# Score tiles by image in two attention stages, and dense matmuls ahead of every third group's scores

## What is computed

```python
# second attention (causal)
scores = jnp.einsum('bhqd,bhkd->bhqk', q, k) * (1.0 / math.sqrt(D))
scores = jnp.where(causal, scores, -jnp.inf)
att = jax.nn.softmax(scores, axis=-1)
y = jnp.einsum('bhqk,bhkd->bhqd', att, v)
# third attention (a scale for each head; a token doesn't look at itself)
attn = jnp.einsum('bhid,bhjd->bhij', q, k) * scale[None, :, None, None]
attn = jnp.where(diag[None, None, :, :], -jnp.inf, attn)
attn = jax.nn.softmax(attn, axis=-1)
out = jnp.einsum('bhij,bhjd->bhid', attn, v)
```

## Time and profile before

| | |
|---|---|
| median of 3 runs | 2166.01 us (2151.96 to 2166.42) |
| profiled execution | 2172.53 us |
| its span, first to last instruction | 2170.6 us |
| TensorE matmuls busy | 1868.5 us (86%), 12440 instructions |
| TensorE weight loads busy | 1723.5 us (79%) |
| VectorE busy | 1134.4 us (52%) |
| ScalarE busy | 799.2 us (37%) |
| GpSimd busy | 588.7 us (27%) |
| mean granted TensorE clock | 0.817 |
| DMA | 151.00 MB, mean 70 GB/s |

### The profile page before, as it was taken

One profiled execution on the slowest core, in us unless ns is written; L12 is line 12 of the kernel. 1 busy time (PEld: TensorE's weight loads), 2 busy tenths in 40 slices (PEclk: granted clock), 3 DMA queues, 4 the chain that ended last, 5 costly groups with the idle time before them and its releaser, 6 DMA issues.

```text
span 2170.6 us, 35211 instructions
## 1 busy us (share of the span) xinstructions
PE 1868.5 (86%) x12440; PEld 1723.5 (79%) x12440; DVE 1134.4 (52%) x3189; ACT 799.2 (37%) x1907; POOL 588.7 (27%) x1369
## 2 busy tenths in 40 slices
PE   7999999996938997998999888977998999889980
PEld 7999888876937777988898778876888898788870
DVE  2423245554327554675577643345775577643436
ACT  1211124323414333553454334434454454334420
POOL 3333241231046433123422310025313412310021
PEclk8855557657966656998998899998999999799995
DMA  4039400003420000001000046651001000046630
GB/s 117 18 107 286 138 1 15 14 24 91 163 78 23 1 15 27 1 1 56 15 2 14 27 139 199 210 170 33 4 1 55 16 1 14 13 150 203 203 107 28
DMA packets 77409, 151.00 MB, mean 70 GB/s; under 512 B 6344, under 2 KB 56626, under 8 KB 77141
## 3 DMA queue, kind: packets, MB, share of 16 engines
q1 hardware_dynamic: 70902, 136.49, 19.7%
q0 software_dynamic: 6336, 12.26, 2.0%
HBM read 108.67 MB, written 41.05 MB: 69 GB/s over the span
## 4 chain that ended last, share of the span: by engine, by line
PE 52%; issue 16%; DVE 14%; DMA 6%; POOL 4%; SPq 3%; ACT 3%; another core or an unknown queue 0%; DVEq 0%; POOLq 0%; ACTq 0%
PE ps_proj L1020 9%; PE ps_o L1075 7%; PE ps_pt L994 6%; DMA w_in<-w_all_dram 5%; PE ps_proj L1095 5%; PE ps_score L1053 4%; PE ps_proj L1033 4%; PE ps_score L1166 4%; PE ps_proj L1149 3%; PE ps_proj L947 2%; SPq L823 2%; ACT w_hi L1281 1%; PE ps_score L968 1%; DVE prob L1439 1%; DVE negmax L1438 1%
## 5 line engine op out<-in xcount | busy, mean ns | idle before, releaser
L1166 PE MATMUL ps_score<-w,hid 128*112 128x192 f32 (+2 forms) x1680 | 306.3, 335 | 14.1 <-DVE x L1717 6.2
L1166 PEld LDWEIGHTS ps_score<-w,hid 128*112 128x112 f32 (+2 forms) x1680 | 278.0, 180 | 16.8 <-issue 8.5
L1330 POOL TENSOR_SCALAR tmp<-rs,var 111x1 f32<-111x1 f32 x154 | 55.4, 360 | 855.9 <-DVE rs L1410 855.4
L1260 ACT ACTIVATE probt<-ps_pt 111x333 f32<-111x333 f32 x308 | 137.8, 447 | 338.7 <-PE ps_pt L994 336.6
L994 PE MATMUL ps_pt<-const,prob 111*111 111x111 f32 x924 | 198.8, 335 | 52.6 <-ACT probt L1260 40.6
L1271 ACT ACTIVATE hid<-ps_proj 128x224 f32<-128x224 f32 (+2 forms) x360 | 133.6, 382 | 265.9 <-PE ps_proj L1149 252.4
L994 PEld LDWEIGHTS ps_pt<-const,prob 111*111 111x111 f32 x924 | 150.0, 223 | 89.7 <-issue 54.5
L1075 PEld LDWEIGHTS ps_o<-v,probt 111*111 111x111 f32 x1584 | 213.5, 215 | 1.1 <-issue 0.5
L1075 PE MATMUL ps_o<-v,probt 111*111 111x65 f32 (+1 forms) x1584 | 208.1, 282 | 0.0
L1318 POOL DMA_INDIRECT tin<-rows_out,idx x66 | 68.0, 1030 | 499.8 <-issue 384.0
L1255 ACT ACTIVATE prob<-prob 111x333 f32<-111x333 f32 x308 | 145.8, 477 | 62.9 <-DVE prob L1439 57.6
(11 more groups left out here) (239 smaller groups left out, 4381.0 us busy)
## 6 DMA issues: line engine op xcount, KB each, us to landing
w_in<-w_all_dram SPq DMA_DIRECT2D x66, 768.0 KB, 4.4
w<-w_all_dram SPq DMA_DIRECT2D x50, 576.0 KB, 5.2
rows_in<-w_lo SPq DMA_DIRECT2D x1, 12320.0 KB, 64.5
rows_out<-w_lo SPq DMA_DIRECT2D x1, 9240.0 KB, 90.1
tin<-rows_in SPq DMA_DIRECT2D x36, 224.0 KB
rows_out<-tout SPq DMA_DIRECT2D x36, 168.0 KB
patch<-patches_dram SPq DMA_DIRECT2D x11, 333.0 KB, 3.2
wo<-wo_all_dram SPq DMA_DIRECT2D x6, 576.0 KB, 3.8
```

The lines of the kernel that those rows point to most:

```text
L1166: last = pe.matmul(bank[0:n, 0:C], hid[:, i % 2, m, at:at + n], w2[:, slot, m, :], start=(m == 0), stop=(m == FC - 1))
L1260: act.activation(probt[:, n % 4, :, :], ps_pt[0:TG, 0:3 * TG].rearrange("p (c n) -> p c n", c=3), ACT.Copy).then_inc(pt_taken, 1)
```

## The change

Both stages (`self.short`) get one score tile a group. The queries of a head are written three times as wide: for each group, image and half chunk, a block of 64 rows by 111 columns, in which columns h x 37 to (h + 1) x 37 hold the rows of head h and zeros elsewhere (a ScalarE copy with a scale that is zero on the other heads' rows). One product with the 37 keys of that image gives three heads' scores for it. So the tile is 111 rows (three heads of 37 queries) by 2 banks x 222 columns (half, image, key); nothing pairs tokens of different images. The probabilities need four transposes, the value products have 37 stationary columns and 51 moving ones (17 for each image, zero outside the token's own image), the outputs stand on 37 rows, and OT takes six transposes. Ahead of the scores of groups 1, 4, 7 and 10 TensorE does twelve products of 128 x 512 with whatever the weight buffer holds, into the bank that the mask then overwrites.

```diff
+        self.short = a in (CAUSAL, DIAG)
-        self.chunks = H // self.per_chunk
+        self.chunks = 2 if self.short else H // self.per_chunk
...
-        _n = 3 if ATTS[_st[1]].t5 else 2
+        _n = 3 if ATTS[_st[1]].t5 else 1
...
+def short_order(a, last_stage, follower):
+
+    out = first_block(a) if last_stage[0] == "ffn" else []
+    for n in range(G + 1):
+        slots = short_fill(a, n, last_stage, follower)
+        if n < G:
+            out.append(("S", n, 0))
+        out += slots[0]
+        if n:
+            out.append(("PV", n - 1, 1))
+        if n < G:
+            out.append(("E", n, 0))
+        out += slots[1]
+        if n < G:
+            out.append(("PT", n, 0))
+        if n:
+            out.append(("OT", n - 1, 0))
+        out += slots[2]
+        if n:
+            out.append(("Y", n - 1))
+        out += slots[3]
...
+                        if g % 3 == 1:
+
+                            full = w1_hi[:, LOAD0[st] % W_RING, :, :].rearrange("p c n -> p (c n)")
+                            for _ in range(12):
+                                pe.matmul(banks[0], full[:, 0:128], full[:, 0:512], start=True, stop=True,
+                                          skip_group_check=True)
                         for bank in banks:
-                            pe.matmul(bank[0:TG, 0:3 * TG], identb[:], maskb[:, a, :, :].rearrange("p h k -> p (h k)"),
+                            pe.matmul(bank[0:TG, 0:2 * TG], identb[:],
+                                      maskb[:, a, 0:2, :].rearrange("p h k -> p (h k)"),
                                       start=True, stop=False, skip_group_check=True)
+                        for j in range(2):
+                            for i in range(IPG):
+                                for e, bank in enumerate(banks):
+                                    at, col = 64 * e, (j * IPG + i) * NTOK
+                                    ins = pe.matmul(bank[0:TG, col:col + NTOK],
+                                                    short_q(b % 2)[at:at + 64, j, g - BLOCKS[b][0], i, :],
+                                                    short_k(b % 2)[at:at + 64, j, t0 + i * NTOK:t0 + (i + 1) * NTOK],
+                                                    start=False, stop=True, skip_group_check=True)
...
+                        for h in range(H):
+
+                            at = (h // 3 % 2 * 2 + h // 6) * TG + h % 3 * NTOK
+                            col = h % 6 * wide
+                            last = pe.matmul(ps_o[0:NTOK, h // 6, col:col + wide], turned_p[:, at:at + NTOK],
+                                             vimg[:, g % 2, h * wide:(h + 1) * wide], start=True, stop=True,
+                                             skip_group_check=True)
...
+                        for h in range(3):
+
+                            ins = act.activation(short_q(b % 2)[:, j, 0:BLOCKS[b][1], :, h * NTOK:(h + 1) * NTOK], src,
+                                                 ACT.Copy, scale=hscale[:, a - CAUSAL, j, h:h + 1])
...
+                        for i in range(IPG):
+
+                            ins = act.activation(dst[:, :, i, 0:s.d], src, ACT.Copy, scale=image[:, i:i + 1])
...
+            def short_shift(st, g):
+
+                _, taken, value = take_score((st, "S", g, 0, 1))
+                scores = ps_score[0:TG, :, 0:2 * TG].rearrange("p e (s k) -> p e s k", k=NTOK)
+                peak = negmax[:].rearrange("p (e s) -> p e s", e=2)
+                link(dve.tensor_reduce(peak, scores, AX.X, ALU.max, negate=True))
+                dst = short_ring(prob, unit(st[1], g, 0)).rearrange("p (e s k) -> p e s k", e=2, k=NTOK)
+                tell(dve.tensor_tensor(dst, scores, peak.unsqueeze(3).to_broadcast([TG, 2, 6, NTOK]), ALU.add),
+                     taken, value, 2)
...
+            def later_fill():
+
+                n = DISPATCH[2].units * DISPATCH[2].width // TL
+                sp.dma_start(rows_in[2].rearrange("k r n -> (k r) n").rearrange("(p t) n -> p t n", p=TL),
+                             zero[:].unsqueeze(1).to_broadcast([TL, n, CX])).then_inc(later_zero, 16)
+                sp.dma_start(rows_out[2].rearrange("k r n -> (k r) n").rearrange("(p t) n -> p t n", p=TL),
+                             zero[:, 0:C].unsqueeze(1).to_broadcast([TL, n, C])).then_inc(later_zero, 16)
+
             for st, step in PROGRAM:
                 kind = step[0]
                 if kind == "W1":
                     next_load(step[1] + 1)
+                    if step[1] == LOAD0[("att", T5)] + 1:
+                        later_fill()
```

More of the change, by code:

```diff
@@ L171, in first_block @@
     s = ATTS[a]
-    return [("QK", 0, j) for j in range(s.qk)] + [("V", 0, j) for j in range(s.vparts)]
+    return [("QK", 0, j) for j in range(s.qk)] + [("V", 0, j) for j in range(0 if s.short else s.vparts)]
 def neigh_order():
@@ new lines, in short_order @@
+def short_order(a, last_stage, follower):
[10 more added lines that the diff above has]
+        out += slots[1]
+        if n < G:
+            out.append(("PT", n, 0))
[5 more added lines that the diff above has]
+        out += slots[3]
+    if a == DIAG:
+        out += [("N2", g) for g in range(G) if ("N2", g) not in out]
+    return out
@@ L314, in att_order @@
     out += [("OT", G - 1, last), ("Y", G - 1)]
-    if a == DIAG:
-        out += [("N2", g) for g in range(G) if ("N2", g) not in out]
     return out
@@ L681, in tower @@
         score_full = sem("score_full")
-        score_taken = [sem(f"score_taken{i}") for i in range(2)]
+        score_taken = sem("score_taken")
         shifted = sem("shifted")
@@ L992, in turn_prob @@
                     pe.wait_ge(pt_taken, n)
-                for i in range(3):
-                    last = pe.transpose(ps_pt[0:TG, i * TG:(i + 1) * TG], prob[:, n % 4, i, :], ident)
+                for i in range(4 if ATTS[a].short else 3):
+                    src = short_ring(prob, n)[:, i * TG:(i + 1) * TG] if ATTS[a].short else prob[:, n % 4, i, :]
+                    last = pe.transpose(ps_pt[0:TG, i * TG:(i + 1) * TG], src, ident)
                 last.then_inc(pt_full, 1)
@@ L1389, in link, with tell @@
                 dve.wait_ge(dve_step, steps[0])
-            def tell(ins, which, value):
-                ins.then_inc(which, 1)
+            def tell(ins, which, value, by=1):
+                ins.then_inc(which, by)
                 dve.wait_ge(which, value)
@@ L1562, in _ @@
                         link(dve.memset(v64[:, :, :, T5_D:T5_D + 1], 1.0))
-                    for e in range(2):
-                        softmax_shift(st, step[1], 2 * step[2] + e, (*key, e))
+                        for r in range(2):
+                            ones = vimg[:, r, :].rearrange("p (h i d) -> p h i d", h=H, i=IPG)[:, :, :, SMALL_D]
+                            link(dve.tensor_copy(ones, image.unsqueeze(1).to_broadcast([TG, H, IPG])))
+                    if ATTS[st[1]].short:
+                        short_shift(st, step[1])
+                    else:
+                        for e in range(2):
+                            softmax_shift(st, step[1], 2 * step[2] + e, (*key, e))
                 elif kind == "PV" and st[1] != NEIGH:
@@ L1802, in lay_out @@
     gw = twice(gw.reshape(C, 3 * E)).reshape(128, 2, 3, E)
-    hs = np.repeat(f["L1_attn_scale"], 32).reshape(3, 128).T
+    hs = np.zeros((2, 4, SMALL_D, 2, 2, 3), np.float32)
+    for a, scale in enumerate((np.full(H, float(SMALL_D) ** -0.5), f["L1_attn_scale"])):
+        for h in range(H):
+            hs[h // 3 % 2, h % 3, :, a, h // 6, h % 3] = scale[h]
+    hs = hs.reshape(128, 2, 2, 3)
     rel = np.arange(NTOK)[None, :] - np.arange(NTOK)[:, None]
@@ L1834, in lay_out, with thirds @@
          for i in range(2) for at in (0, SMALL_D)] + [with_bias(w[:, 2 * C:], b[0, 2 * C:])], 1)
-    def wide(w):
-        return np.concatenate([w, np.zeros((C, F - w.shape[1]), np.float32)], 1)
+    def thirds(w):
+        out = np.zeros((C, 2, 2, 4, SMALL_D), np.float32)
+        out[:, :, :, 0:3, :] = w.reshape(C, 2, 2, 3, SMALL_D)
+        return out.reshape(C, 256)
     maps, outs = [], []
@@ L1841, in lay_out @@
         w = w.T
-        maps += [np.concatenate([spread(w[:, 0:C], 0), spread(w[:, C:2 * C], 0)], 1), wide(w[:, 2 * C:])]
+        maps.append(np.concatenate([thirds(w[:, 0:C]), thirds(w[:, C:2 * C]), w[:, 2 * C:],
+                                    np.zeros((C, F - SHORT_V - C), np.float32)], 1))
         padded = np.concatenate([wo.T, np.zeros((F - C, C), np.float32)])
```

232 lines of the change are left out of this document (167 added, 65 removed).

## The result

| | before | changed |
|---|---|---|
| median | 2158.99 us (4 runs, 2133.29 to 2166.42) | 2020.21 us (4 runs, 1999.13 to 2052.00) |
| profiled execution, span | 2172.5, 2170.6 us | 2052.0, 2050.2 us |
| mean granted clock | 0.817 | 0.851 |
| first attention (from 35 us) | 280.8 us | 247.1 us |
| second attention | 168.0 us | 137.0 us |

Some executions of one and the same kernel are slower as a whole, at a lower granted clock: the ratios leave them out, the medians don't, and the changed kernel's profiled execution (2052.0 us) is one of them. Later, beside other runs of the kernel before, the changed kernel took 1998.9 and 1992.5 us, 0.9306 (0.9241 to 0.9371) and 0.9294 (0.9246 to 0.9341).

The account below looks back on a forecast made before the run. The two stages were taken as bound by TensorE's own list at its granted clock. Savings 29 + 28 + 22 = 79 us from 2172.5 gave 2093.5, 2087 by the median, said 2085; own range 2060 to 2112, 8 in 10 2033 to 2130.

Parts of the forecast that it names:

- (b): Ahead of the second and third attention: one weight load less, removing 4.3 us lost by TensorE at each.
- A second term: Third attention: 27 us less, and 1 from the next stage's projections standing in the last group's waits.
- The clock of the first attention: Between 109.4 and 314 us TensorE had 200.3 busy us of 204.6, all at clock 0.50.
- price of the value products: Both stages, 24 instructions a group: 4.26 to 2.04 us at half clock, 2.20 to 1.3 at full.
- The scores: Both stages, twelve products a group with 37 moving columns instead of 111: no gain taken, at most 1.9 us at half.
- the waits: Per group 0.3 us more at half clock, 0.9 at full; third attention 4 us more for inputs from GpSimd.
- One sign of being wrong: In the changed stages: TensorE waits over 2 us a group for the exponential or the division.
- The dense products: Ahead of groups 1, 4, 7, 10: cost 18.4 us a stage; with QK, full-clock groups rise 5 to 7.5, 4 to 6.
- a mere cost: Second and third attention: dense runs raise the clock too late or too briefly; 58 us saved, 2108; chance 0.20.
- clock full nearly throughout: Second and third attention at full clock: 54 and 57 us less, 2033 in all; chance 0.12.
- (a): Two QK chunks and V leave each first block: 4.1 and 3.2 us saved.
- (c): Router's tail: one logit and count fewer, a fourth of its first 15 us, 3.7 us saved.

Follow-up runs that it names:

- The kernel with dense products: Kernel before, plus only twelve 128 x 512 products ahead of groups 1, 4, 7 and 10 in second and third attention: 2148.5 us, 0.9974.
- the two later groups: Second and third groups of runs: changed kernel unaltered, run again beside the kernel before (2147.8 and 2148.3 us): 1998.9 and 1992.5 us.

## Why the prediction was right and wrong

**Right:** the direction, and the cause as far as the two stages go. Second attention: 139 us said, 137.0 measured. Masks, transposes and value products together were to save 41.7 us in the second and 44.4 in the third; they saved 41.9 and 44.1. The unchanged rest took 1332.4 and 1332.7 us in the first pair of profiles (over all fourteen profiles 1316.5 to 1332.7), and no wait came from the fills in the third attention (79.3 us until the second has landed, with the output weights 8.7 us behind their issue).

**The step that failed is (b), one load less ahead of the second attention.** I took what TensorE lost in the profiled execution, 4.3 us, as the price of the load behind the fills. That was the price at half clock. ScalarE had waited 17.5 us for the weights already, which I didn't weigh, and the issue and the transfer stood 92 us in the chain: the end of the stage was bound by two things at once, TensorE at half clock and the load, and TensorE's wait shows only their difference. The kernel with dense products shows the same wait as 37.2 us. Taking the load out of the queue's way alone gave 55 to 60 us (ratios 0.9728 and 0.9758), so the term should have been some 55 instead of 4.3. The profiles show 43 of it in the first attention (252.2 us with the wait, 208.1 and 209.6 without) and 71 to 73 against the 280.8 us of the kernel before, of which there is one profile; where the rest of the 55 to 60 lies stays open.

**A second term was too small: the third attention.** 28 us less were said, 47.8 measured (189.9 to 142.1, both with the fourth's first projections; the "near 147" of the prediction leaves these 14 us out, its sum gives 162 with them). 13 of the 20 lie in the stage without its dense products and some 7 in these, as the table and the paragraph behind it show.

**The clock of the first attention** I read as fixed from one execution, "at half from 109 to 314 us". Over fourteen profiled executions of this stage it took 199 to 281 us with nearly the same list: 281 and 252 in the two with the load behind the fills, 199 to 270 in the others. In the changed kernel's first profile the clock was at half for 160 of its 247 us; in the two later ones the stage took 216 and 210 us, at half for 96 and 82. That this is also what separates the first median, 2020, from the later 1992 and 1999 is likely, but only one of the first four executions was profiled.

**Second and third attention.** Between the kernel before and the first run of the changed kernel without dense products the terms can be laid side by side; the measured ones are sums over the timeline, from each instruction's start to the next, so that a wait counts with the row ahead of it.

| us saved in the stage | second: said | measured | third: said | measured |
|---|---|---|---|---|
| masks | 8.6 | 7.4 | 9.0 | 8.6 |
| scores | 0 | 1.4 | 0 | 4.0 |
| probability transposes | 15.4 | 16.9 | 16.4 | 20.2 |
| value products | 17.7 | 17.6 | 19.0 | 15.3 |
| output transposes | -5.1 | 0.3 | -5.4 | -3.4 |
| QK | 6.5 | 5.2 | 7.5 | 7.7 |
| other waits and the rest | -7 | -6.6 | -9 | -1.8 |
| whole stage | 36 | 42.2 | 37.5 | 50.6 |

These savings hold what the clock gave too, which was 0.68 instead of 0.66 in the second and 0.69 instead of 0.64 in the third. The price of the value products is hit: 1.22 us at full and 2.19 at half for 24 instructions, where 1.3 and 2.04 were taken. The Trainium skill's rule for weight loads (TensorE: Matmul & The Clock Gate, "LDWEIGHTS") gives 31 ns for 37 columns and no floor; with the floor of 62 ns that the prediction set beside it they would take 1.5 us at either clock. The trace disagrees: 51 ns an instruction at full clock are below that floor, and 91 at half show that the price follows the clock. Two terms were too dear. The scores do cost less with 37 moving columns than with 111: 100 ns each at half (2.39/24), 116 before (1.39/12), 54 at full against 64. And in the third attention the waits hardly grew, 14.8 to 18.8 idle us without the dense products, though I had charged 10: of the inputs from combines only one kept TensorE waiting, 2.8 us. With the dense products, and more of the stage at full clock, they are 23.8 us. Waits of TensorE in the third attention of the changed kernel, from its first mask on: us in total, times, longest.

```profile
PE ps_pt L1093 <- ACT prob L1407: 8.5, 6, 3.0
PE ps_proj L1217 <- DVE o L1622: 5.1, 8, 2.5
PE ps_proj L1234 <- ACT ot L1393: 3.4, 7, 0.6
PE ps_turn L990 <- POOL x L1498: 2.8, 1, 2.8
```

One sign of being wrong does show here: TensorE waited up to 3.0 us for an exponential and 2.5 us for a division, where over 2 us were named. Over the eleven groups that is 13.6 us, 1.2 a group.

**The dense products** took 19.8 and 17.4 us in the first profile, 18.4 said. By the working on record they were to pay 18.4 in each stage and give back 11.3 (2.5 groups at 4.5) and 9: a loss of 7 and 9 us. Against the kernel without them they lost 11 and 3 in the first profile, nothing in the last, and 8 in the medians of one group, which noise could cover. So this step was right in sign, as far as can be told, but not by its mechanism. The QK behind the run was to hold the clock into group 3; in the first profile it fell 7 to 10 us behind the runs, and the clock came out at 0.72 where 0.80 was said (0.82 where 0.75 was said in the third). In the third attention the clock was at half between the first dense run and the next QK, which the prediction both allowed for and names as a sign of being wrong. The rival "a mere cost" (2108) has part of this right, the clock that falls soon, but not the cost: of 19.8 and 17.4 us some 9 and 15 came back. Its remark on the rule stands: the Trainium skill (TensorE: Matmul & The Clock Gate, "Why this matters for your kernels") has a continuously busy engine at full clock; TensorE was busy 65.00 of 65.00 us and 75.00 of 75.00 at 0.50 in the changed kernel's first attention. The trace disagrees. The rival "clock full nearly throughout" adds up to 116 us for the second stage and not 114, which changes nothing.

**Around them.** (a) QK0 was 1.1 us shorter, 3.2 said. (b) ahead of the third: the stage before is 5.9 us shorter, 4.3 said. (c) The router's tail is 1.7 us shorter, 3.7 said.

**What made up the gain.** In the two later groups the changed kernel is 149 and 156 us under the kernel before. The forecast's 79, with 51 more for the load and 20 more for the third attention, are 150. By the runs: short tiles with all that hangs on them give some 100 (2095.9 to 1995.0, the load out of the fills' shadow in both), the load 55 to 60, and the dense products take some 8 back. The 139 us of the first medians are less; the first attention was long in the one execution of them that was profiled. Not settled: why that stage is granted more half clock in some executions than in others; no change of its own products is shown to alter it.

## What to carry to other kernels

A wait of 4 us can stand in front of a floor of 50: where the engine that waits is itself slowed in that execution (here by the clock), add up the other chain, from the queue's first blocked issue to the landing, and ask when the stage could end if the engine were at full speed. Put a weight load ahead of large fills in an in-order queue. Raising the clock with work that computes nothing is judged by the stage's time, never by the clock: 0.87 with it was slower than 0.68 without. And one profile of a kernel whose clock moves is one draw: take a second before pricing a wait from it.

## What the runs showed of the hardware

- The granted clock of the same code differs between executions: the first attention of the changed kernel took 247.1, 215.6 and 209.9 us in three profiles, at 0.68, 0.78 and 0.81, and its second 136.7 and 125.4 us in the two later ones, at 0.72 and 0.80.
- A run of twelve f32 products of 128 x 512 that began at half clock (seven of eight in the first profile) ended with the clock full or rising within 1 us; it then stayed full for 7 to 10 us among small f32 products, in one later execution for 48 us.
- f32 products with 111 stationary columns on 64 rows and 37 moving columns take 54 ns an instruction at full clock and 100 at half; with 37 stationary and 51 moving columns 51 and 91 ns. Their price follows the clock nearly in full.
- A fill of 12.3 and one of 9.2 MB beside the first attention (0.46 of DMA share) cost TensorE nothing that shows, when no load waits behind them: 208.1 us with them, 209.6 without.
